# Building the adjacency matrices of a graph network: paired values for VectorE, degree sums as rows of one PSUM bank, ranks carried by groups of four tiles

## The chip, the cores and the metric

The kernel runs on one core of a Trainium2 chip. The metric is the device time of one execution in microseconds (us). TensorE (PE), VectorE (DVE), ScalarE (ACT), GpSimd (POOL) and SyncE (SP) run side by side and wait for each other by semaphores.

## The reference

Four graph layers are applied in turn to 6250 nodes of 128 features, with 106250 directed edges sorted by destination:

```
x = _layernorm(x + _L0_gnn_ref(x, edge_index, edge_attr_64, ...))   # message MLP per edge, summed per node, GRU
x = _layernorm(x + _L1_gnn_ref(x, edge_index, ...))                 # deg^-1/2 normalized sum over edges and reversed edges
x = _layernorm(x + _L2_gnn_ref(x, edge_index, ...))                 # the same over edges
x = _layernorm(x + _L3_gnn_ref(x, edge_index, edge_weight, ...))    # three weighted convolutions
```

A layer of this kind is a product of a node-by-node matrix with the features, scaled by powers of the nodes' degrees:

```
deg = jax.ops.segment_sum(w, dst, num_segments=n_nodes)
msg = m[src] * norm[:, None]
out = jax.ops.segment_sum(msg, dst, num_segments=n_nodes)
```

## The kernel before

The nodes make NB = 49 blocks of 128. One stage builds, once, three dense matrices (edge counts, reversed counts, edge weights) block row by block row, stores them in HBM, and later stages multiply with them. The change lies in this building stage, which runs from about 60 to about 1600 us; it also carries the first graph layer (one gather of node rows, one small product and one sum for each of 208 steps of 512 edges), woven between the block work at places that are fixed in the code (`at_place`, `tick`).

For block row u, DVE and PE sort the edges of the block (at most 20 tiles of 128 edges) so that each edge stands alone in a slot of its pair k of source blocks (NK = 25 pairs):

- `sort_keys(u)` (L617, L619) marks for every edge its pair: `in_pair`, 20 tiles by 26.
- `ranks(u)` on PE (L778, L780) counts, for each edge, the earlier edges of its pair: one product with a triangle, then 19 products that carry the sum of tile t to all later tiles.
- `sort_ranks(u)` on DVE (L626 to L640) makes `at_rank` (where each edge goes) and `spread` (its five values times `in_pair`, L634).
- `sort(u)` on PE (L788) moves them to their slots; `sort_out(u)` on DVE (L646 to L652) reads the result into `slots`.
- `one_hots(u, h)` on DVE builds for the two halves h of the pairs the one-hot matrices: `hot_s` of the sources (L665, 25 instructions a row), `hot_d` of the destinations (L670), and for u >= NARROW = 16 three weighted ones `hot_w` (L677). `hot_d` and `hot_w` lie in the room called `rows_a` in the profile.
- `blocks(n)` on PE takes one or two pairs a step, 13 steps a row. For each pair: products for the matrices (L814, L817), and sums for the degrees with the one-hots as the stationary operand and 1 or 4 columns moving (L815, L819). For u >= 16 twelve products more for the weights (L834).
- ACT takes each PSUM bank to SBUF (L904, L909), SP stores it. There are three banks (`ps_mat`) and three staging buffers.

The rows u < 16 ("narrow") leave out the forward counts and the weights; the rows u >= 16 are called wide here. First-layer work on the same engines: POOL gathers rows of `p_table` (L925, four for each step, eight steps ahead at most), PE multiplies (L844) and sums (L857), DVE adds and places (L685, L689, L697, L698), ACT applies ReLU (L914). Each engine works its own list in the order of the code.

Of the kernel before, what the change touches and what calls it, by code (L numbers as in the profile page):

```python
# [59 lines left out]
FAR = 1e6  # L60
assert CHUNKS * CB == NB and CHKS * CHK == NB and E <= T * P and HS * TH == T and HS % 2 == 0
# [48 lines left out]
def per_row(col, n):  # L110

    return col.unsqueeze(2).to_broadcast([col.shape[0], col.shape[1], n])

# [12 lines left out]
def build(nc, a, out):  # L126
    with ExitStack() as ctx:
# [43 lines left out]
        zero = sb("zero", [P, 64 + 4 * NB])  # L171
# [55 lines left out]
        with ExitStack() as c:  # L227
# [14 lines left out]
            with ExitStack() as c0:  # L242
# [50 lines left out]
                with nc.Block() as block:  # L293
# [67 lines left out]
                    def _(dve):  # L361
# [32 lines left out]
                        chain.step(V.tensor_scalar(vals[:, :, 1], dst_row[:], 1.0, None, ALU.add))  # L394
# [33 lines left out]
                        chain.step(V.tensor_tensor(vals[:, :, 0], tmp_f[:], src_f[:], ALU.subtract))  # L428
# [83 lines left out]
            spread = sb("spread", [P, VT, NV, NK + 1], BF16, c)  # L512

            slots = sb("slots", [P, 2, NV + 1, NK + 1], BF16, c)
# [10 lines left out]
            hot = sb("hot", [P, 4, TH, W], F32, c)  # L525
            st_cnt = sb("st_cnt", [P, STAGES, 2, 4 * P], BF16, c)
            st_wt = sb("st_wt", [P, STAGES, 4 * P], F32, c)
            deg_in = sb("deg_in", [P, NB, 4], F32, c)
            deg_out = sb("deg_out", [P, NB], F32, c)
            self_c = sb("self_c", [P, NB], F32, c)  # L530
            self_w = sb("self_w", [P, NB], F32, c)
            deg = sb("deg", [P, 4, NB], F32, c)
# [8 lines left out]
            hot_d_ready, source_ready = sem("hot_d_ready"), sem("source_ready")  # L541
            hots_ready, filled, evicted = sem("hots_ready"), sem("filled"), sem("evicted")
# [62 lines left out]
            with nc.Block() as block:  # L605
                @block.vector
                def _(dve):
# [5 lines left out]
                    def sort_keys(u):  # L613
# [6 lines left out]
                                        ALU.is_equal).then_inc(pair_ready, 1)  # L620

                    def sort_ranks(u):
# [11 lines left out]
                        V.tensor_tensor(spread[:], in_pair[:].unsqueeze(2).to_broadcast([P, VT, NV, NK + 1]),  # L634
                                        vals[:, at, :].unsqueeze(3).to_broadcast([P, VT, NV, NK + 1]),
# [64 lines left out]
                    def tick():  # L700
# [3 lines left out]
                        if e is not None:  # L704
                            if e < HS:
                                message_sum(e)
                            if e >= 4 and e % 2 == 0:
                                add_sums((e - 4) // 2)

                    sort_keys(0)  # L710
                    sort_ranks(0)
                    sort_out(0)
# [1318 lines left out]
```

## Time and profile before

| | us |
|---|---|
| median of 3 runs | 4412.11 (4409.29 to 4418.47) |
| profiled execution, its own time | 4412.28 |
| its span | 4410.5 |
| PE busy | 3810.4 (86%) |
| DVE busy | 2944.6 (67%) |
| POOL busy | 2815.0 (64%) |
| ACT busy | 1529.5 (35%) |

Shares of the whole span average over stages with different limits; the building stage is about a third of the span and has to be read by itself. A matmul's recorded duration holds its way through the array, so the pace of PE is read from the starts of its instructions.

In a row of the windows stand the stretch, its length, busy us (and instructions) of PE, PE's weight loads, DVE, ACT and POOL, TensorE's granted clock (1.00 is 2.4 GHz, 0.50 is 1.2 GHz), the share of the DMA engines and GB/s. In a row of groups: busy us, mean ns of one, idle us ahead of them and what ended it. In a row of a timeline: start and duration in us.

### The profile page before, as it was taken

The page shows a single profiled execution, that of the slowest core. Times are in us where ns is not written, and L with a number is a line of the kernel's source. Part 1 is how long each engine was busy: PE and PEld are TensorE (multiplying, and loading weights), DVE is VectorE, ACT ScalarE, POOL GpSimd, SP SyncE. Part 2 cuts the span into 40 slices and gives each one's busy share as a digit, 9 for nine tenths or more (in the row PEclk, how much of TensorE's full clock was granted, in tenths as well). Part 3 has the DMA queues.
Part 4 walks back from the last instruction along what each step waited for, and adds up shares of the span by engine and source line. Part 5 has one row for each costly group of instructions (what it writes and reads, how often), then busy time and mean ns, then how long its engine had stood idle before and what let it go on. Part 6 is the DMA issues. An engine that isn't in the chain of part 4 may idle for free. (4 is left out here: it accounts for less than half of the span.)

```text
span 4410.5 us, 83016 instructions
## 1 busy us (share of the span) xinstructions
PE 3810.4 (86%) x30818; PEld 2546.0 (58%) x30818; DVE 2944.6 (67%) x6093; ACT 1529.5 (35%) x3170; POOL 2815.0 (64%) x2363
## 2 busy tenths in 40 slices
PE   5887999998988865688987986999899999998998
PEld 4766888887878754344444443455445555554444
DVE  8899999999999868355553344466356666523665
ACT  3334566665656546000000000333134444412332
POOL 3876888888888810566635774777266666606773
PEclk7778999998999977899998998999999999998999
DMA  4444777777777753999976775999655555537997
GB/s 140 133 126 133 231 247 240 238 237 225 248 236 238 228 201 115 290 322 322 323 260 211 240 233 167 329 323 327 219 204 195 185 199 191 193 109 278 331 318 263
DMA packets 612904, 1019.51 MB, mean 231 GB/s; under 512 B 90888, under 2 KB 417575, under 8 KB 612111
## 3 DMA queue, kind: packets, MB, share of 16 engines
q1 hardware_dynamic: 476700, 773.91, 51.5%
q0 software_dynamic: 90848, 199.74, 15.3%
q10 hardware_dynamic: 44956, 40.55, 2.8%
q8 instruction: 247, 4.05, 0.4%
q14 instruction: 153, 1.25, 0.1%
HBM read 737.12 MB, written 276.78 MB: 230 GB/s over the span
## 5 line engine op out<-in xcount | busy, mean ns | idle before, releaser
L925 POOL DMA_INDIRECT x<-p_table,src_i x832 | 1218.5, 1464 | 344.5 <-issue 241.8
L1514 POOL DMA_INDIRECT rows_b<-x_table,low_src x552 | 574.9, 1041 | 485.1 <-POOLq L144 206.4
L1514 POOL DMA_INDIRECT rows_a<-h_table,low_src x412 | 448.1, 1088 | 240.1 <-DVE split_l3b L1805 120.4
L904 ACT CAST st_cnt<-ps_mat 128x512 bf16<-128x512 f32 (+1 forms) x825 | 440.9, 590 | 444.5 <-PE ps_deg L819 384.3
L1593 PE MATMUL po_l3b<-mat_l3b,rows_b 128*128 128x512 f32 (+1 forms) x1372 | 570.9, 564 | 19.6 <-DMA mat_l3b<-weights_fwd 18.6
L1593 PE MATMUL po_l3a<-mat_l3a,rows_a 128*128 128x512 f32 (+1 forms) x882 | 375.0, 572 | 30.0 <-DMA mat_l3a<-weights_fwd 29.3
L1593 PE MATMUL po_l3c<-mat_l3c,rows_a 128*128 128x512 f32 (+1 forms) x882 | 375.3, 573 | 13.9 <-DMA mat_l3c<-weights_fwd 13.2
L1593 PE MATMUL po_l<-mat_l,rows_a 128*128 128x512 bf16 (+1 forms) x1323 | 296.2, 380 | 99.8 <-DVE mat_l L1833 99.0
L1593 PEld LDWEIGHTS po_l3b<-mat_l3b,rows_b 128*128 128x128 f32 x1372 | 241.6, 195 | 241.5 <-issue 221.1
L834 PE MATMUL ps_mat<-rows_a,hot_s 128*128 128x128 bf16 x4851 | 360.8, 226 | 9.0
L677 DVE TENSOR_TENSOR rows_a<-rows_a,slots 128x1792 bf16<-128x1792 bf16 (+1 forms) x198 | 366.8, 1886 | 1.4
L1514 POOL DMA_INDIRECT rows_a<-x_table,low_src x276 | 285.7, 1035 | 93.3 <-issue 84.5
L1514 POOL DMA_INDIRECT rows_a<-m_table,low_src x276 | 276.9, 1003 | 90.2 <-issue 85.0
L814 PE MATMUL ps_mat<-rows_a,hot_s 128*128 128x128 bf16 x1617 | 255.5, 224 | 88.0 <-DVE rows_a L677 64.7
L1748 ACT ACTIVATE t_l<-y_l 128x512 f32<-128x512 f32 (+1 forms) x26 | 15.7, 605 | 887.7 <-DVE y_l L1888 887.7
L817 PE MATMUL ps_mat<-hot_s,rows_a 128*128 128x256 bf16 x1225 | 321.8, 284 | 0.0
L834 PEld LDWEIGHTS ps_mat<-rows_a,hot_s 128*128 128x128 bf16 x4851 | 291.2, 101 | 46.2 <-ACT st_wt L909 34.8
L1593 PE MATMUL po_l<-mat_l,rows_b 128*128 128x512 bf16 (+1 forms) x1323 | 289.2, 374 | 19.3 <-DMA mat_l<-counts_fwd 18.4
L815 PE MATMUL ps_deg<-slots,hot_s 128*128 128x1 bf16 x2401 | 283.7, 168 | 22.7 <-issue 13.3
L844 PE MATMUL pm<-w1eT,rows_a 65*128 65x128 f32 x1664 | 254.3, 300 | 13.9 <-DVE x L689 13.8
L1593 PEld LDWEIGHTS po_l<-mat_l,rows_a 128*128 128x128 bf16 x1323 | 123.8, 102 | 242.4 <-DVE mat_l L1833 112.3
L1593 PEld LDWEIGHTS po_l3a<-mat_l3a,rows_a 128*128 128x128 f32 x882 | 157.9, 196 | 176.2 <-issue 145.6
(415 smaller groups left out, 7448.8 us busy)
## 6 DMA issues: line engine op xcount, KB each, us to landing
weights_fwd<-st_wt SPq DMA_DIRECT2D x396, 256.0 KB
mat_l<-counts_fwd SPq DMA_DIRECT2D x112, 896.0 KB
mat_l3a<-weights_fwd SPq DMA_DIRECT2D x56, 1792.0 KB
mat_l3c<-weights_fwd SPq DMA_DIRECT2D x56, 1792.0 KB
counts_rev<-st_cnt SPq DMA_DIRECT2D x588, 128.0 KB
rev_l<-counts_rev SPq DMA_DIRECT2D x84, 896.0 KB
mat_l3b<-weights_fwd SPq DMA_DIRECT2D x42, 1792.0 KB
counts_fwd<-st_cnt SPq DMA_DIRECT2D x396, 128.0 KB
```

Of the source, the lines that this page charges most:

```text
L677: V.tensor_tensor(hot_w[:, h, v, 0:n, :], hot_d[:, h, 0:n, :], per_row(slots[:, u % 2, 2 + v, ks], P), ALU.mult).then_inc(hots_ready, 1)
L814: nc.tensor.matmul(ps_mat[:, b, q * P:(q + 1) * P], half, rows, start=True, stop=True)
L815: nc.tensor.matmul(ps_deg[:, 2 * k + q:2 * k + q + 1], half, slots[:, u % 2, NV, k:k + 1], start=False, stop=False)
L817: nc.tensor.matmul(ps_mat[:, b, rev_at:rev_at + len(halves) * P], rows, hot_s[:, h, j0 + j, 0:len(halves) * P], start=True, stop=True)
L834: mm = nc.tensor.matmul(ps_mat[:, f % 3, (2 * j + q) * P:(2 * j + q + 1) * P], half, hot_w[:, h, v, j0 + j, :], start=(v == 0), stop=(v == 2))
L844: mm = nc.tensor.matmul(pm[:, j % 2, t * FD:(t + 1) * FD], edge[:, i % 2, (h * TH + t) * P:(h * TH + t + 1) * P], w1eT[:], start=True, sto ...
L904: nc.scalar.copy(st_cnt[:, q, :, j * 2 * P:j * 2 * P + n_col], ps_mat[:, f % 3, :].rearrange("p (d c) -> p d c", d=2)[:, :, 0:n_col]).then ...
L925: pool.indirect_dma_start(ring[:, j % RING, t * FD:(t + 1) * FD], None, p_table, bass.IndirectOffsetOnAxis(src_i[:, j * TH + t:j * TH + t ...
L1514: pool.indirect_dma_start(ring[:, j % RL, t, :], None, table, bass.IndirectOffsetOnAxis(low_src[:, j * TH + t:j * TH + t + 1].bitcast(U32), 0)
L1593: mm = nc.tensor.matmul(po[:, p % 2, k, 0:nb * P].rearrange("p (d c) -> p d c", c=P), rows[:, s, k * P:(k + 1) * P], cols, start=(s == 0 a ...
L1748: nc.scalar.activation(t1[:, 0:nb, 0:FD], y2[:, f % ys, 0:nb], ACT.Square).then_inc(act_out, 1)
```

## The change

Five edits, all in the building stage.

1. `hot_d`, `hot_w` and `spread` multiply or compare a tile with a value that is the same for a whole row. Before, that value is read with a step of zero, element by element. Now each value lies twice side by side (`slots` and `vals_2` hold every value two times), and the operand is read as pairs of neighbours.
2. The degree sums. Before, the one-hot matrix is stationary and one or four columns move, and each sum is a column of `ps_deg`. Now a small matrix `marks` is stationary (its k+1 or 4 row+4 columns are zero but for the last ones), the one-hot matrices move (256 and 128 columns), and each sum is a row of `ps_deg`. `marks` is filled by a new copy for each half row and zeroed once.
3. The ranks. DVE sums `in_pair` over groups of four tiles (`group_sum`), and PE carries inside the groups by three products and from group to group by four.
4. At the end of the stage ACT copies `ps_deg` to SBUF and PE turns it by four small products; DVE reads the turned sums.
5. The order of the five values changes, and some buffers share room.

```
 def twice(col):
     return col.unsqueeze(len(col.shape)).to_broadcast([*col.shape, 2])
 def in_pairs(tile):
     return tile.rearrange("p n (c e) -> p n c e", e=2)
 def per_row_pairs(pairs, n):
     return pairs.unsqueeze(2).to_broadcast([pairs.shape[0], pairs.shape[1], n // 2, 2])
...
+                        dve.wait_ge(pair_ready, u + 1)
+                            V.tensor_reduce(group_sum[:], in_pair[:, 0:VT - 4, 0:NK].rearrange("p (g t) k -> p g k t", t=4),
+                                            AX.X, ALU.add).then_inc(groups_ready, 1)
...
+                        V.tensor_copy(vals_2[:], twice(vals[:, at]))
...
-                        V.tensor_tensor(spread[:], in_pair[:].unsqueeze(2).to_broadcast([P, VT, NV, NK + 1]),
-                                        vals[:, at, :].unsqueeze(3).to_broadcast([P, VT, NV, NK + 1]),
+                        V.tensor_tensor(spread[:].rearrange("p t v (k e) -> p t v k e", e=2),
+                                        in_pair[:].rearrange("p t (k e) -> p t k e", e=2).unsqueeze(2).to_broadcast(
+                                            [P, VT, NV, (NK + 1) // 2, 2]),
+                                        vals_2[:].unsqueeze(3).to_broadcast([P, VT, NV, (NK + 1) // 2, 2]),
                                         ALU.mult).then_inc(lots_ready, 1)
...
-                        V.tensor_copy(slots[:, u % 2, 0:NV, :], found).then_inc(slots_ready, 1)
+                        V.tensor_copy(slots[:, u % 2], twice(found)).then_inc(slots_ready, 1)
...
-                        V.tensor_scalar(slots[:, u % 2, NV, :], slots[:, u % 2, 1, :], 0.0, None,
+                        V.tensor_scalar(slots[:, u % 2, 1], slots[:, u % 2, 0], 0.0, None,
                                         ALU.is_gt).then_inc(slots_ready, 1)
...
-                        V.tensor_tensor(hot_d[:, h, 0:n, :], per_block(iota_up[:], n), per_row(slots[:, u % 2, 1, ks], P),
+                        dve.wait_ge(slots_ready, 2 * u + 2)
+                        V.tensor_copy(marks[:, ks.start:min(ks.stop, NK), LEAD:], slots[:, u % 2, 1:NV, ks.start:min(ks.stop, NK), 0].rearrange(
+                            "p v k -> p k v")).then_inc(marks_ready, 1)
+                        V.tensor_tensor(in_pairs(hot_d[:, h, 0:n, :]), in_pairs(per_block(iota_up[:], n)),
+                                        per_row_pairs(slots[:, u % 2, 0, ks], P),
                                         ALU.is_equal).then_inc(hot_d_ready, 1)
...
-                            V.tensor_tensor(hot_w[:, h, v, 0:n, :], hot_d[:, h, 0:n, :],
-                                            per_row(slots[:, u % 2, 2 + v, ks], P), ALU.mult).then_inc(hots_ready, 1)
+                            V.tensor_tensor(in_pairs(hot_w[:, h, v, 0:n, :]), in_pairs(hot_d[:, h, 0:n, :]),
+                                            per_row_pairs(slots[:, u % 2, 2 + v, ks], P), ALU.mult).then_inc(hots_ready, 1)
...
+                    V.memset(marks[:], 0.0).then_inc(marks_ready, 1)
...
-                        for t in range(VT - 1):
-                            mm = nc.tensor.matmul(at[:, t + 1:VT, :], ones_b[:],
-                                                  in_pair[:, t:t + 1, 0:NK].to_broadcast([P, VT - 1 - t, NK]),
-                                                  start=False, stop=(t == VT - 2))
+                        at_4, pair_4 = (v.rearrange("p (g t) k -> p g t k", t=4) for v in (at, in_pair[:, :, 0:NK]))
+                        for d in range(1, 4):
+                            nc.tensor.matmul(at_4[:, :, d:4, :], ones_b[:], pair_4[:, :, 0:4 - d, :], start=False, stop=False)
+                        pe.wait_ge(groups_ready, u + 1)
+                        for g in range(VT // 4 - 1):
+                            mm = nc.tensor.matmul(at[:, 4 * g + 4:VT, :], ones_b[:],
+                                                  group_sum[:, g:g + 1, :].to_broadcast([P, VT - 4 * g - 4, NK]),
+                                                  start=False, stop=(g == VT // 4 - 2))
...
-                                nc.tensor.matmul(ps_deg[:, 2 * k + q:2 * k + q + 1], half, slots[:, u % 2, NV, k:k + 1],
-                                                 start=False, stop=False)
...
-                            mm = nc.tensor.matmul(ps_deg[:, 64 + 4 * u:68 + 4 * u], rows, slots[:, u % 2, 2:NV + 1, k],
-                                                  start=False, stop=False)
+                            both = hot_s[:, h, j0 + j, 0:len(halves) * P]
+                            nc.tensor.matmul(ps_deg[0:k + 1, 0:len(halves) * P], marks[:, k, LEAD - k:LEAD + 1], both,
+                                             start=False, stop=False)
+                            nc.tensor.matmul(ps_deg[0:4 * row + 4, (2 + part) * P:(3 + part) * P],
+                                             marks[:, k, LEAD - 4 * row:LEAD + 4], rows, start=False, stop=False)
...
+                    nc.scalar.copy(deg_sums, ps_deg[:]).then_inc(degs_copied, 1)
```

What TensorE does for the first pair of a wide row, before (the names are the tile written, then the two operands; the shape is that of the moving operand):

```order
L814 MATMUL ps_mat<-rows_a,hot_s 128x128
L815 MATMUL ps_deg<-slots,hot_s 128x1
L814 MATMUL ps_mat<-rows_a,hot_s 128x128
L815 MATMUL ps_deg<-slots,hot_s 128x1
L817 MATMUL ps_mat<-hot_s,rows_a 128x256
L819 MATMUL ps_deg<-slots,rows_a 128x4
```

and at the same place after (block row 16; the first number of a shape on `marks` is the number of its columns that are stationary):

```order
L854 MATMUL ps_deg<-hot_s,marks 1x256
L856 MATMUL ps_deg<-rows_a,marks 68x128
L860 MATMUL ps_mat<-rows_a,hot_s 128x128 x2
L862 MATMUL ps_mat<-hot_s,rows_a 128x256
L854 MATMUL ps_deg<-hot_s,marks 2x256
```

Six products a pair became five, and the degree sums moved ahead of the matrix products, with 384 moving columns where there were 6.

The ranks on TensorE, before (first rows of 20):

```order
L778 MATMUL ps_sort<-in_pair,tri_b 128x500
L780 MATMUL ps_sort<-in_pair,ones_b 128x475
L780 MATMUL ps_sort<-in_pair,ones_b 128x450
L780 MATMUL ps_sort<-in_pair,ones_b 128x425
L780 MATMUL ps_sort<-in_pair,ones_b 128x400
```

and after, all of them:

```order
L816 MATMUL ps_sort<-in_pair,tri_b 128x500
L819 MATMUL ps_sort<-in_pair,ones_b 128x5x75
L819 MATMUL ps_sort<-in_pair,ones_b 128x5x50
L819 MATMUL ps_sort<-in_pair,ones_b 128x5x25
L822 MATMUL ps_sort<-group_sum,ones_b 128x400
L822 MATMUL ps_sort<-group_sum,ones_b 128x300
L822 MATMUL ps_sort<-group_sum,ones_b 128x200
L822 MATMUL ps_sort<-group_sum,ones_b 128x100
```

Twenty products of 5250 columns became eight of 2250, and the last four wait for a sum that VectorE makes.

On VectorE, the end of the first half's one-hots and the start of the next row's sort, before (square brackets name the semaphores that a row waits for):

```order
L677 TENSOR_TENSOR rows_a<-rows_a,slots 128x1792 x2
L685 TENSOR_TENSOR hot<-iota_row,local 128x256 [waits step_sum]
L689 TENSOR_TENSOR x<-pm,x 128x512 [waits edge_mul,gathered3]
L626 TENSOR_TENSOR picked<-in_pair,ps_sort 128x500 [waits pair_ready,ranked]
L628 TENSOR_REDUCE rank<-picked 128x20 [waits b_dve]
```

and after (`vals<-vals` is the copy into `vals_2`):

```order
L712 TENSOR_TENSOR rows_a<-rows_a,slots 128x1792 x2
L720 TENSOR_TENSOR hot<-iota_row,local 128x256 [waits step_sum]
L724 TENSOR_TENSOR x<-pm,x 128x512 [waits edge_mul,gathered3]
L654 ISA [waits pair_ready,ranked]
L654 COPY vals<-vals 128x200
L655 TENSOR_TENSOR picked<-in_pair,ps_sort 128x500
L657 TENSOR_REDUCE rank<-picked 128x20 [waits b_dve]
```

The old instructions keep their order and their sizes; copies are set in between, here behind the wait for the ranks.

## Rows read from the trace of the kernel before

**Rows 1.** Windows: the narrow block rows, then the wide ones

```profile
60.00:425.00 365.00, 286.32 (x2959) 237.78 (x2960) 327.57 (x848) 130.61 (x250) 271.87 (x200) 0.78 0.43 124
425.00:1590.00 1165.00, 1055.85 (x13547) 951.19 (x13545) 1084.47 (x2088) 705.94 (x1405) 945.54 (x632) 0.93 0.74 235
```

**Rows 2.** Who waited for whom, 425 to 1590 us: us, times, longest

```profile
ACT st_cnt L904 <- PE ps_deg L819: 384.3, 192, 8.3
...
PE ps_mat L814 <- DVE rows_a L677: 64.7, 29, 5.7
ACT st_cnt L904 <- DMA weights_fwd<-st_wt: 46.9, 45, 2.7
...
DVE key L617 <- issue: 21.0, 31, 1.5
...
DVE acc L697 <- issue: 16.2, 21, 1.4
PE ps_mat L814 <- ACT st_cnt L904: 14.9, 41, 2.2
DVE x L689 <- DMA x<-p_table,src_i: 14.1, 10, 2.5
...
PE pm L844 <- DVE x L689: 11.5, 9, 3.0
...
PE ps_mat L814 <- DVE hot_s L665: 5.4, 9, 1.4
```

**Rows 3.** Groups of DVE by shape, 425 to 1590 us: busy us, mean ns | idle

```profile
L677 DVE TENSOR_TENSOR rows_a<-rows_a,slots 128x1792 bf16<-128x1792 bf16 x98 | 194.4, 2019 | 0.6
L677 DVE TENSOR_TENSOR rows_a<-rows_a,slots 128x1536 bf16<-128x1536 bf16 x99 | 170.3, 1753 | 0.8
...
L634 DVE TENSOR_TENSOR spread<-in_pair,vals 128x2600 bf16<-128x2600 bf16 x32 | 91.5, 2861 | 0.0
...
L631 DVE TENSOR_TENSOR at_rank<-num_r,rank_b 128x2560 bf16<-128x2560 bf16 x32 | 47.7, 1492 | 1.1
...
L628 DVE TENSOR_REDUCE rank<-picked 128x20 f32<-128x500 f32 x32 | 21.6, 674 | 1.1
...
L646 DVE CAST slots<-ps_sort 128x130 bf16<-128x130 f32 x32 | 9.2, 287 | 0.0
```

**Rows 4.** Groups of POOL, the same stretch

```profile
L925 POOL DMA_INDIRECT x<-p_table,src_i x632 | 945.5, 1496 | 200.6 <-issue 183.9 <-DVE x L689 16.7
```

**Rows 5.** Timeline of DVE and of POOL near 1040 us: start, us

```profile
1038.49 1.75 DVE L670 TENSOR_TENSOR rows_a<-iota_up,slots 128x1536 bf16<-128x1536 bf16 x1
...
1038.56 2.50 POOL L925 DMA_INDIRECT x<-p_table,src_i  x1 [0.30 <-issue]
1041.37 0.94 POOL L925 DMA_INDIRECT x<-p_table,src_i  x1 [0.30 <-issue]
```

**Rows 6.** Timeline of PE: ranks, then steps, then a first-layer piece

```profile
1018.11 0.38 PE L778 MATMUL ps_sort<-in_pair,tri_b 128*128 128x500 bf16 x1
...
1020.51 0.22 PE L814 MATMUL ps_mat<-rows_a,hot_s 128*128 128x128 bf16 x1
...
1020.80 0.22 PE L814 MATMUL ps_mat<-rows_a,hot_s 128*128 128x128 bf16 x1
...
1021.77 0.22 PE L814 MATMUL ps_mat<-rows_a,hot_s 128*128 128x128 bf16 x1
...
1023.34 1.11 PE L844 MATMUL pm<-w1eT,rows_a 65*128 65x128 f32 x8
```

**Rows 7.** Groups of DVE by shape, 60 to 425 us

```profile
L634 DVE TENSOR_TENSOR spread<-in_pair,vals 128x2600 bf16<-128x2600 bf16 x17 | 48.6, 2860 | 0.0
L670 DVE TENSOR_TENSOR rows_a<-iota_up,slots 128x1792 bf16<-128x1792 bf16 x17 | 34.2, 2015 | 0.0
...
L670 DVE TENSOR_TENSOR rows_a<-iota_up,slots 128x1536 bf16<-128x1536 bf16 x16 | 28.0, 1748 | 0.0
...
L626 DVE TENSOR_TENSOR picked<-in_pair,ps_sort 128x500 f32<-128x500 bf16 x17 | 11.4, 669 | 13.8 <-PE ps_sort L780 13.8
```

More of the change, by code:

```diff
@@ L60 @@
 FAR = 1e6
+DEG_BLOCKS = -(-NB // 2)
+LEAD = 4 * (DEG_BLOCKS - 1)
 assert CHUNKS * CB == NB and CHKS * CHK == NB and E <= T * P and HS * TH == T and HS % 2 == 0
@@ L112, in per_row, with twice, in_pairs, per_row_pairs @@
     return col.unsqueeze(2).to_broadcast([col.shape[0], col.shape[1], n])
+def twice(col):
+    return col.unsqueeze(len(col.shape)).to_broadcast([*col.shape, 2])
+def in_pairs(tile):
+    return tile.rearrange("p n (c e) -> p n c e", e=2)
+def per_row_pairs(pairs, n):
+    return pairs.unsqueeze(2).to_broadcast([pairs.shape[0], pairs.shape[1], n // 2, 2])
 def per_block(row, k):
@@ L512, in build @@
             spread = sb("spread", [P, VT, NV, NK + 1], BF16, c)
-            slots = sb("slots", [P, 2, NV + 1, NK + 1], BF16, c)
+            vals_2 = sb("vals_2", [P, VT, NV, 2], BF16, c)
+            slots = sb("slots", [P, 2, NV, NK + 1, 2], BF16, c)
             source = sb("source", [P, 2, NK + 1], F32, c)
@@ L620, in sort_keys @@
                                         ALU.is_equal).then_inc(pair_ready, 1)
+                        dve.wait_ge(pair_ready, u + 1)
+                        with nc.allow_low_precision(reason="whole numbers up to four"):
+                            V.tensor_reduce(group_sum[:], in_pair[:, 0:VT - 4, 0:NK].rearrange("p (g t) k -> p g k t", t=4),
+                                            AX.X, ALU.add).then_inc(groups_ready, 1)
                     def sort_ranks(u):
@@ L799, in blocks @@
                         pe.wait_ge(hot_d_ready, m + 1)
-                        if s == 0:
-                            pe.wait_ge(slots_ready, 2 * u + 2)
+                        pe.wait_ge(marks_ready, m + 2)
+                        part, row = divmod(u, DEG_BLOCKS)
                         for j, k in enumerate(sub_pairs(s)):
@@ L886, in _ @@
                             first_layer(u, s)
-                    nc.tensor.matmul(ps_deg[:, 0:DEG], zero[:, 0:P], zero[:, 0:DEG], start=False, stop=True).then_inc(filled, 1)
+                    nc.tensor.matmul(ps_deg[:], zero[:, 0:P], no_sums, start=False, stop=True).then_inc(filled, 1)
+                    pe.wait_ge(evicted, fills_before(NB))
+                    pe.wait_ge(degs_copied, 1)
+                    for part in range(2):
+                        n = 4 * min(DEG_BLOCKS, NB - part * DEG_BLOCKS)
+                        nc.tensor.matmul(ps_mat[:, 0, 4 * DEG_BLOCKS * part:4 * DEG_BLOCKS * part + n],
+                                         deg_sums[0:n, (2 + part) * P:(3 + part) * P], ident[0:n, 0:n], start=True, stop=True)
+                    for q in range(2):
+                        n = NK - (2 * NK > NB and q)
+                        mm = nc.tensor.matmul(ps_mat[:, 1, q:q + 2 * n - 1:2], deg_sums[0:n, q * P:(q + 1) * P],
+                                              ident[0:n, 0:n], start=True, stop=True)
+                    mm.then_inc(degs_turned, 1)
                     pe.wait_ge(count_ready, 1)
@@ L1053, in _ @@
                         act.wait_ge(turned, 1)
-                        nc.scalar.copy(deg_rows[:], ps_mat[0:2 * NB, 0, 0:P]).then_inc(turn_read, 1)
+                        nc.scalar.copy(deg_rows, ps_mat[0:2 * NB, 0, 0:P]).then_inc(turn_read, 1)
                         act.wait_ge(root_in, 1)
```

66 lines of the change are left out of this document (37 added, 29 removed).

## The prediction

> **What bounds the kernel now.** I read the windows first. The building stage is two stretches: 365 us with 16 narrow block rows (some 22 us each, the start included) and 1165 us with 33 wide ones (35.3 us each) [rows 1]. In the wide stretch DVE is busy 1084 of 1165 us, 93%. PE shows 1056, but its durations overlap; ACT is busy 61%, the DMA engines 74%. POOL is busy 946 and idle 201, of which 184 are the 0.30 us between two gathers in which it waits for nobody [rows 4]: 632 x (1.496 + 0.305) = 1138 us, so POOL never rests either.
>
> The waits tell who is late. PE waits for DVE at L814 and L844, 65 + 12 + 5 = 82 us, and for ACT 15 us; DVE waits for a gather only 14 us, and its other idle time (21 + 16 us) is the reading of registers [rows 2]. ACT's 384 us behind PE are its slack. So DVE sets the pace of the wide rows, with POOL 27 us behind it. In the narrow stretch DVE is busy 328 of 365 us, and 14 of the rest are waits for the ranks [rows 1, 7].
>
> **Why DVE and POOL are tied.** Near 1040 us DVE runs L670 for 1.75 us; a gather that POOL starts 0.07 us later takes 2.50 us, and the next one 0.94 [rows 5]: 1.75 - 0.07 + 0.82. So a gather that meets a long two-input operation of DVE waits for its end. The mean of 1.496 us [rows 4] is 0.94 and 0.56 of such waiting. Shorter operations on DVE therefore make POOL faster too.
>
> The Trainium skill ("SBUF — State Buffer", Who interferes with whom) says that a Vector instruction with two SBUF inputs contends with a GpSimd instruction that reads SBUF, and infers that descriptor generation is not held up by it. The first half fits the 2.50 us, the second does not; if it held for these gathers, they would keep their 1.496 us.
>
> **Edit 1, pairs.** Per element, L677 costs (2019 - 1753) / 256 = 1.04 ns, with 157 ns fixed [rows 3]. `at_rank` (L631) has both inputs with neighbours side by side and takes 1.492 us for 2560 elements, 0.52 ns each [rows 3]. No row has a pair repeated 64 times. Upper bound: nothing gained, 2.02 us stays. Lower bound: L631's rate, 157 + 1792 x 0.52 = 1.09 us, 0.96 for 1536, 1.51 for `spread`. I take the lower one: the old operand is a repeated element too and runs at the full 1.04 ns, so repeating costs nothing.
> - Wide: L677 98 x 0.93 + 99 x 0.79 = 169 us; L670, at the durations of [rows 7] and 33 of each, 0.92 x 33 + 0.79 x 33 = 56; `spread` 32 x 1.35 = 43 [rows 3]. Together 268.
> - Narrow: 17 x 0.92 + 16 x 0.79 + 17 x 1.35 = 51 us [rows 7].
>
> **What DVE gets in return**, per block row: the group sum reads 400 elements; L628 reads 500 in 0.674, so 0.57 us if its strided reading is free, and I allow 1.1 at twice that; the copy to `vals_2`, 200 elements, 0.25 (L646 takes 0.287 for 130 out of PSUM, so 0.36 at most); `slots` written twice, 130 elements more than L646's 0.287, 0.14; two copies of about 50 elements to `marks`, 0.2 each by the same row; waits and the doubled comparison 0.1. Sum 1.5 us (up to 2.1): 49 us wide, 25 narrow. Zeroing `marks` (2500 columns) is up to 2.6 us once. DVE's wide work falls by 268 - 49 = 219 to about 946 us for the stretch, idle time included. So DVE stops being the bound, and what comes next has to be found.
>
> **POOL next?** The waiting of a gather goes as the sum of squared durations of the two-input operations over the row's time. Per wide row that sum was 4 x (2.02² + 1.75²) + 2.86² + 1.49² + 1.6 (small ones) = 41; it becomes 4 x (1.09² + 0.96²) + 1.51² + 1.49² + 1.6 = 14.6. Even in a row 9% shorter the waiting falls to 0.39 of 0.56 = 0.22 us: 632 x (0.94 + 0.22 + 0.305) = 926 us. POOL does not bind.
>
> **PE is next** (edits 2 and 3). The ranks take 20 products, 1018.11 to 1020.51, 2.40 us for 5250 columns [rows 6]. Now 8 products of 2250 columns, 0.43 of it, 1.03 us; 31 rows x 1.37 = 43 us. Part of this time was used by ACT to catch up, so I count 32. For each pair, six products from 1020.51 took 0.29 us to the next pair's first at 1020.80 [rows 6]. At 2.40 us / 5250 = 0.457 ns per column the new pair's 896 columns are 0.41 us at most, and 0.37 at 2.4 GHz; 0.08 more in 816 pairs, 68 us, if nothing hides it. But ACT hides most: the first step after the ranks takes 1.26 us (1020.51 to 1021.77), the second 1.57 (to 1023.34) [rows 6], since ACT must first empty a bank. Two such steps with 0.16 us more each are 2.84 us instead of 2.83. A row has 13 steps and about 7 pieces between them (5 of the first layer, one sort, one ranks), so some two or three steps a row stand alone and pay: 2.5 x 0.16 x 33 = 13 us.
>
> The wide stretch is then 1165 - 82 (waits for DVE) + 17 (a rest of them, since DVE at 946 is near) - 32 + 13 - 18 = 1063 us. The 18 are for the clock: granted 0.93 [rows 1], so 14% of the stretch, 163 us, ran at 1.2 GHz after PE had waited; the most that this can give back is half of it, 82 us, the least nothing; I take 18, since much of it lies beside waits that are counted already, and since PE will still wait now and then. So -102.
>
> **Narrow rows.** DVE 51 - 25 = 26 us less; of the 14 us of waits for ranks half goes, 7; the zeroing takes 2.6 back; and PE, at a clock of 0.78 there [rows 1], has 640 moving columns for each pair where it had 262, for which I take 10 back. -20 us.
>
> **The end** (edit 4): a copy of 512 columns on ACT, four small products and two copies, all beside some 13 us of DVE's own work behind the same semaphore. Nothing; if it were all on the path, 2 us.
>
> Sum, against the profiled execution's 4412.3 (the median is 4412.1): 4412 - 102 - 20 = 4290; I say 4288.
>
> **The rivals.**
> - ACT and the stores hold the wide rows. ACT already waits 47 us for stores to land [rows 2], and DMA engines busy 0.74 go above 0.8. Then the ranks give nothing and a quarter of PE's 82 us of waits for DVE turns into waits for ACT, so 60 are left: 4412 - 60 - 20 = 4332. Chance 0.13.
> - Repeated pairs cost something: the operations take the middle of the two bounds, 1.55 us. DVE saves 134 - 49 = 85 us wide and nothing narrow, and the zeroing costs 2.6: 4330. Against it stands the free repeat of one element today. Chance 0.08. The Trainium skill ("Vector Engine (DVE) Microarchitecture Reference", Measured stream behaviour) says that a port keeps its rate only for runs of two adjacent 4-byte words, 1.73 instead of 1.05 ns otherwise. By that figure a product would take some 1.7 us; a pair of two-byte values is one such word.
> - Gathers keep 1.496 us: POOL binds at 1138 of 1165, total 4412 - 27 - 20 = 4365. Against it: the 2.50 and 0.94 us. Chance 0.05.
> - DVE's bound is all there is, PE follows: wide 946 + 25, total 4200. Chance 0.04.
> - Slower, and the change not doing what it says: pairs run at 1.04 ns an element as before. Then DVE, the bound, has 1.5 us more in each of 49 rows and 2.6 once: 4412 + 76 = 4488. It decides once the pairs save less than a fifth (49 of 268). L631 speaks against it. Chance 0.06.
>
> **How the numbers follow.** My forecast has 0.62, with its own range 4225 to 4330 (cost of the group sum, clock, ACT's share). 0.02 is left for no change. 0.2% of this time, 9 us, is about what a measurement can tell. The range 4225 to 4350 leaves out the slower case, the POOL case, the lowest and some of my own. Faster 0.92, same 0.02, slower 0.06.
>
> **What would show it.** L677's successor at 1.09 us (1792) and `spread` at 1.51. Gathers at a mean near 1.15. DVE busy near 80% in the wide rows, with waits for PE's `filled`; PE's waits for DVE under 20 us, its clock over 0.95. A wide row near 32 us, a narrow one near 20. Wrong would be: products over 1.3 us, PE's new degree products spaced wider than their columns, or ACT's waits for stores beyond 100 us.

## The result and the profile after

The changed kernel takes 4379.22 us, median of 4 runs (4375.57 to 4382.22); the kernel before, on the same chip, takes 4415.2 (4409.29 to 4418.47). The ratio is 0.9922, interval 0.9906 to 0.9938: 0.8% faster where 2.8% was forecast, and outside the range on its upper side. The profiled execution took 4380.14 us, its span is 4378.0.

By its interval the kernel is faster, but by less than the 2% that this study calls faster.

First the windows of the changed kernel, narrow rows and wide ones, with the columns of [rows 1]:

```profile
60.00:400.00 340.00, 328.46 (x2339) 205.00 (x2340) 301.08 (x914) 133.98 (x247) 220.77 (x199) 0.96 0.45 131
400.00:1560.00 1160.00, 1156.71 (x12482) 915.54 (x12479) 873.38 (x2219) 754.72 (x1418) 713.32 (x632) 1.00 0.75 238
```

In the wide rows DVE fell from 93% [rows 1] to 75% busy and POOL from 81% to 61%. PE went from 1056 of 1165 to 1157 of 1160 us, at a granted clock of 1.00. The bound has moved to PE, and PE has more to do than DVE had. Its waits, 400 to 1560 us (us, times, longest), are gone:

```profile
PE ps_deg L854 <- ACT st_cnt L958: 1.8, 4, 0.8
PE ps_deg L854 <- DVE rows_a L704: 0.7, 1, 0.7
PE ps_deg L854 <- ACT st_wt L963: 0.2, 1, 0.2
```

The groups of DVE by shape and of POOL, same stretch, which answer to [rows 3] and [rows 4]:

```profile
L712 DVE TENSOR_TENSOR rows_a<-rows_a,slots 128x1792 bf16<-128x1792 bf16 x98 | 103.0, 1084 | 0.6
L712 DVE TENSOR_TENSOR rows_a<-rows_a,slots 128x1536 bf16<-128x1536 bf16 x99 | 91.3, 955 | 0.8
L663 DVE TENSOR_TENSOR spread<-in_pair,vals 128x2600 bf16<-128x2600 bf16 x32 | 48.1, 1504 | 0.0
L647 DVE TENSOR_REDUCE group_sum<-in_pair 128x100 bf16<-128x400 bf16 x31 | 25.9, 835 | 1.1
L677 DVE CAST slots<-ps_sort 128x260 bf16<-128x260 f32 x32 | 13.6, 426 | 19.7 <-PE ps_sort L830 15.8 <-issue 3.8
L980 POOL DMA_INDIRECT x<-p_table,src_i x632 | 713.3, 1129 | 377.6 <-DVE x L724 203.1 <-issue 174.5
```

The pairs take 1084, 955 and 1504 ns, within a hundredth of a us of the lower bound, and the gathers 1129 ns. POOL now waits 203 us for a free buffer. So DVE and POOL did what was forecast. PE did not. The stationary operand of a product is the one that PE loads ahead of it (the weight load, PEld in the profile); the other one is the moving operand, and its columns set how long the product streams. The timeline of PE in two pieces: the degree products have 13 and 8 stationary columns in the first, 7 and 36 in the second (start, us; the first number behind the names is partitions by stationary columns, the next the moving shape):

```profile
771.85 0.28 PE L854 MATMUL ps_deg<-hot_s,marks 128*13 128x256 bf16 x1
771.97 0.22 PE L856 MATMUL ps_deg<-rows_a,marks 128*8 128x128 bf16 x1
772.12 0.28 PE L860 MATMUL ps_mat<-rows_a,hot_s 128*128 128x128 bf16 x2
772.24 0.27 PE L862 MATMUL ps_mat<-hot_s,rows_a 128*128 128x256 bf16 x1
772.44 0.28 PE L854 MATMUL ps_deg<-hot_s,marks 128*14 128x256 bf16 x1
...
1003.87 0.27 PE L854 MATMUL ps_deg<-hot_s,marks 128*7 128x256 bf16 x1
1004.07 0.23 PE L856 MATMUL ps_deg<-rows_a,marks 128*36 128x128 bf16 x1
1004.23 0.28 PE L860 MATMUL ps_mat<-rows_a,hot_s 128*128 128x128 bf16 x2
1004.36 0.27 PE L862 MATMUL ps_mat<-hot_s,rows_a 128*128 128x256 bf16 x1
1004.56 0.27 PE L854 MATMUL ps_deg<-hot_s,marks 128*8 128x256 bf16 x1
```

Read the starts. A pair takes 0.59 us in the first piece and 0.69 in the second; before it took 0.29 [rows 6], and 0.41 was the forecast's most. Where a product of 256 moving columns is followed by one of like width the next start is 0.12 us later (771.85 to 771.97, 13 to 8 columns). Where the width goes from 7 to 36 it is 0.20 (1003.87 to 1004.07). The same 0.20 stands behind L862 (772.24 to 772.44, 1004.36 to 1004.56), where 128 stationary columns are followed by 8 or 14. The weight loads of the same two pieces say why (start, us, stationary columns):

```profile
771.86 0.09 PEld L856 LDWEIGHTS ps_deg<-rows_a,marks 128*8 128x8 bf16 x1
772.12 0.11 PEld L860 LDWEIGHTS ps_mat<-rows_a,hot_s 128*128 128x128 bf16 x2 [0.17 <-issue]
772.19 0.10 PEld L862 LDWEIGHTS ps_mat<-hot_s,rows_a 128*128 128x128 bf16 x1
...
1004.07 0.09 PEld L856 LDWEIGHTS ps_deg<-rows_a,marks 128*36 128x36 bf16 x1
1004.23 0.11 PEld L860 LDWEIGHTS ps_mat<-rows_a,hot_s 128*128 128x128 bf16 x2
1004.30 0.10 PEld L862 LDWEIGHTS ps_mat<-hot_s,rows_a 128*128 128x128 bf16 x1
1004.56 0.08 PEld L854 LDWEIGHTS ps_deg<-hot_s,marks 128*8 128x8 bf16 x1 [0.16 <-ACT st_wt L963]
```

Of like width, a load runs while the product ahead still streams: the load for the product at 771.97 begins at 771.86, that for 1004.36 at 1004.30. Of another width (8 to 128 at 772.12, 7 to 36 at 1004.07, 128 to 8 at 1004.56) load and product have the same start: the load is not taken ahead, and both start some 0.09 us late. The delay lies ahead of the load's start, so it is not the length of the load; what PE does in it the trace does not show. The widths need not be equal: over all block rows the spacing behind L854 has a median of 113 ns when both widths are 32 or less, and 206 ns when the second is above 32. There seem to be three classes of width (up to 32, up to 64, above 64), and the pair of `marks` columns crosses them two or three times. The experiments were made to test this.

The trace of the changed kernel has every width from 4 to 100 in steps of four, so it also shows where the classes end (medians of the spacing of starts in ns, over the pairs of wide rows that have another pair right behind them; e3 and e4 are explained below):

| columns of L856 | L854 to L856 | L856 to L860 | L862 to the next L854 | the pair |
|---|---|---|---|---|
| 4 to 32 | 113 | 152 | 202 | 590 |
| 36 to 64 | 206 | 164 to 176 | 202 | 695 to 707 |
| 68 to 100 | 206 | 82 to 95 | 202 | 602 to 616 |
| 128 or 100 for both (e3, e4) | 109 | 56 | 109 | 386 |

One border lies between 32 and 36 columns and the other between 64 and 68. The timeline on both sides of the second:

```profile
1291.27 0.24 PE L856 MATMUL ps_deg<-rows_a,marks 128*64 128x128 bf16 x1
1291.44 0.28 PE L860 MATMUL ps_mat<-rows_a,hot_s 128*128 128x128 bf16 x2
...
1325.25 0.24 PE L856 MATMUL ps_deg<-rows_a,marks 128*68 128x128 bf16 x1
1325.33 0.27 PE L860 MATMUL ps_mat<-rows_a,hot_s 128*128 128x128 bf16 x2
```

The table shows a second, smaller cost. Behind a product whose own load was not taken ahead, the next start is later by about 0.4 ns for each of its stationary columns (82 ns with 68 columns, 95 with 100, where 56 is the spacing of hidden loads); with 128 columns it is only 10 ns later (66 instead of 56 between the two L860 of the first two lines).

The ranks, in the timeline of the same kernel: the first of the eight products and what follows the last, 1.10 us apart (2.40 before, [rows 6]).

```profile
501.92 0.38 PE L816 MATMUL ps_sort<-in_pair,tri_b 128*128 128x500 bf16 x1
...
503.02 0.28 PE L854 MATMUL ps_deg<-hot_s,marks 128*21 128x256 bf16 x1
```

The Trainium skill ("TensorE: Matmul & The Clock Gate", Step-by-step: what each phase is for) says that TensorE pulls the load of a stationary operand ahead of running products when their row groups do not conflict, or when the load goes to the background weight buffer. It names no condition on the number of stationary columns for this, and all these products use 128 rows, so by that page nothing tells one of these loads from another. The trace shows loads taken ahead for like width (771.86 for the product at 771.97) and not for the others (772.12 for the product at 772.12): the measurement decides.

### The profile page after: what moved, and what is told of

It is laid out like the page before. It is cut to its first block and busy times, and to the rows that moved or that the text cites. A ratio compares the mean times of both kernels' runs of the same rounds, so it can differ in the third digit from the quotient of the medians.

```text
span 4378.0 us, 80386 instructions
## 1 busy us (share of the span) xinstructions
PE 3946.3 (90%) x29062; PEld 2471.1 (56%) x29062; DVE 2706.7 (62%) x6290; ACT 1577.2 (36%) x3171; POOL 2538.0 (58%) x2363
## 5 line engine op out<-in xcount | busy, mean ns | idle before, releaser
L980 POOL DMA_INDIRECT x<-p_table,src_i x832 | 935.3, 1124 | 545.7 <-DVE x L724 257.2
L958 ACT CAST st_cnt<-ps_mat 128x512 bf16<-128x512 f32 (+1 forms) x825 | 454.4, 578 | 380.7 <-PE ps_mat L862 358.8
L854 PE MATMUL ps_deg<-hot_s,marks 128*1 128x256 bf16 (+4 forms) x1225 | 336.5, 275 | 6.0 <-DVE rows_a L704 3.4
L877 PE MATMUL ps_mat<-rows_a,hot_s 128*128 128x128 bf16 x4851 | 340.9, 219 | 0.0
L862 PE MATMUL ps_mat<-hot_s,rows_a 128*128 128x256 bf16 x1225 | 336.3, 275 | 0.0
L877 PEld LDWEIGHTS ps_mat<-rows_a,hot_s 128*128 128x128 bf16 x4851 | 305.4, 98 | 4.5
L856 PE MATMUL ps_deg<-rows_a,marks 128*4 128x128 bf16 (+24 forms) x1225 | 290.2, 237 | 0.0
L696 DVE TENSOR_SCALAR hot_s<-iota,source 128x256 bf16<-128x256 bf16 x1225 | 253.0, 293 | 38.9 <-PE ps_mat L877 37.8
L1756 ACT ACTIVATE split_l3b<-rows_a,low_weight 128x256 bf16<-128x256 f32 x412 | 175.4, 496 | 213.8 <-DMA rows_a<-h_table,low_src 146.5
```

Of the source, the lines that this page charges most:

```text
L696: V.tensor_scalar(hot_s[:, h, j, :], iota_256[:], source[:, u % 2, k:k + 1], None, ALU.is_equal).then_inc(hots_ready, 1)
L854: nc.tensor.matmul(ps_deg[0:k + 1, 0:len(halves) * P], marks[:, k, LEAD - k:LEAD + 1], both, start=False, stop=False)
L856: nc.tensor.matmul(ps_deg[0:4 * row + 4, (2 + part) * P:(3 + part) * P], marks[:, k, LEAD - 4 * row:LEAD + 4], rows, start=False, stop=False)
L862: mm = nc.tensor.matmul(ps_mat[:, b, rev_at:rev_at + len(halves) * P], rows, both, start=True, stop=True)
L877: mm = nc.tensor.matmul(ps_mat[:, f % 3, (2 * j + q) * P:(2 * j + q + 1) * P], half, hot_w[:, h, v, j0 + j, :], start=(v == 0), stop=(v == 2))
L958: nc.scalar.copy(st_cnt[:, q, :, j * 2 * P:j * 2 * P + n_col], ps_mat[:, f % 3, :].rearrange("p (d c) -> p d c", d=2)[:, :, 0:n_col]).then ...
```

## The experiments

Each run was made beside the kernel before on its chip. Runs e1 to e4 share one chip (before: 4427.18 us), e5 to e8 another (4940.8), e9 to e12 a third (4412.07). "First to last ranks" is the time from the start of the first product of the ranks to that of the last (block row 0 to 48): 1465.8 us before, 1435.3 after.

| run | us, median | ratio (interval) | first to last ranks |
|---|---|---|---|
| changed kernel | 4379.22 | 0.9922 (0.9906 to 0.9938) | 1435.3 |
| e1 pairs and ranks, degrees as before | 4269.7 | 0.9629 (0.9591 to 0.9667) | 1330.5 |
| e2 pairs only | 4273.18 | 0.965 (0.9616 to 0.9684) | 1326.5 |
| e3 marks 128 wide | 4254.36 | 0.961 (0.9576 to 0.9644) | 1312.2 |
| e4 marks 100 wide | 4248.69 | 0.9598 (0.957 to 0.9627) | 1309.4 |
| e9 marks grouped | 4295.25 | 0.9742 (0.971 to 0.9774) | 1354.8 |
| e10 single values | 4464.47 | 1.0126 (1.0093 to 1.016) | 1514.8 |
| e11 e1, stationary cut to 32 | 4717.04 | 1.0717 (1.0673 to 1.0762) | 1761.5 |
| e12 e1, stationary cut to 96 | 4267.88 | 0.9685 (0.9643 to 0.9727) | 1319.9 |

**Which edit takes the gain back.** e1 is the changed kernel with the degree sums of before: one and four moving columns, the one-hots stationary, no `marks`, no turning.

```
-  nc.tensor.matmul(ps_deg[0:k + 1, 0:len(halves) * P], marks[:, k, LEAD - k:LEAD + 1], both, ...)
-  nc.tensor.matmul(ps_deg[0:4 * row + 4, (2 + part) * P:(3 + part) * P], marks[:, k, LEAD - 4 * row:LEAD + 4], rows, ...)
+  nc.tensor.matmul(ps_deg[:, 2 * k + q:2 * k + q + 1], half, slots[:, u % 2, 1, k, 0:1], ...)     # for each q
+  nc.tensor.matmul(ps_deg[:, 64 + 4 * u:68 + 4 * u], rows, slots[:, u % 2, 1:NV, k, 0], ...)
```

Expected:

> The changed kernel with the degree sums as before: the one-hot matrices stationary, 1 or 4 columns of slots moving, no marks, no copy and turn at the end; pairs for VectorE and grouped ranks stay. Theory (the narrow stationary marks cost PE 0.69 us a pair where its columns say 0.37): a pair is back at 0.29 to 0.31 us, the wide rows fall from 35.3 to about 32 us, the total to 4255 to 4290. Rival (what holds the changed kernel is something else that the pairs brought, as ACT's evictions or the stores): the time stays within 20 us of the changed kernel's 4379.

Measured: 4269.7 us, ratio 0.9629, inside the range of the theory. Without edit 2 the kernel is 3% faster than with it.

e2 is edit 1 alone: the degree sums and the 20 products of the ranks as before.

```
-  for d in range(1, 4): ...   # grouped ranks, and group_sum on DVE
+  for t in range(VT - 1):
+      mm = nc.tensor.matmul(at[:, t + 1:VT, :], ones_b[:], in_pair[:, t:t + 1, 0:NK].to_broadcast([P, VT - 1 - t, NK]), ...)
```

Expected:

> The kernel before with edit 1 alone (values twice side by side); ranks and degree sums as before. Theory: PE's 82 us of waits for VectorE go for the most part, 4285 to 4310, 20 to 40 us above the same with grouped ranks. Rival (VectorE's shorter operations were worth nothing by themselves): within 20 us of 4412.

Measured: 4273.18 us, ratio 0.965. That is below the expected 4285 to 4310, and 3.5 us above e1 where 20 to 40 were expected; the intervals of e1 and e2 overlap. So the grouped ranks (edit 3) give nothing that can be told, and edit 1 alone gives 3.5%. The windows of e1 and, below it, of e2 from 400 to 1400 us show where the ranks' gain stays:

```profile
400.00:1400.00 1000.00, 939.27 (x12484) 851.32 (x12482) 816.68 (x2048) 665.71 (x1328) 712.13 (x623) 0.96 0.82 262
```
```profile
400.00:1400.00 1000.00, 953.13 (x12845) 851.97 (x12841) 796.69 (x2027) 665.59 (x1330) 699.84 (x623) 0.99 0.82 262
```

PE is busy 14 us less in e1, and ACT and the DMA engines have done the same work in the same time, so something beside PE's work sets the pace. The waits of e1 (380 to 1470 us) point to ACT and the stores:

```profile
ACT st_cnt L940 <- PE ps_deg L855: 234.5, 140, 8.7
ACT st_cnt L940 <- DMA weights_fwd<-st_wt: 102.3, 92, 3.2
```

ACT waits 102 us for stores to leave a staging buffer, where it waited 47 [rows 2]. PE's clock is a second candidate: 0.96 was granted in e1's stretch and 0.99 in e2's, so part of what the grouped ranks save may come back as slower products. No run separates the two.

**Is it the number of columns, or the change of width?** e3 keeps edit 2, but gives every product on `marks` a stationary operand of 128 columns, mostly zeros: the same 384 moving columns a pair, wider loads, and no change of width. Some small tiles share room with others to make place for the wider `marks`.

```
-  LEAD = 4 * (DEG_BLOCKS - 1)
+  LEAD = DEG_BLOCKS - 1;  WIDE = 128
-  nc.tensor.matmul(ps_deg[0:k + 1, ...], marks[:, k, LEAD - k:LEAD + 1], both, ...)
-  nc.tensor.matmul(ps_deg[0:4 * row + 4, ...], marks[:, k, LEAD - 4 * row:LEAD + 4], rows, ...)
+  nc.tensor.matmul(ps_deg[0:WIDE, ...], marks[:, k, LEAD - k:LEAD - k + WIDE], both, ...)
+  nc.tensor.matmul(ps_deg[0:WIDE, ...], marks[:, k, LEAD - row:LEAD - row + WIDE], rows, ...)
```

Expected:

> The changed kernel with marks stationary always 128 columns wide (152 columns kept for each pair, the four values 25 columns apart, the sums in rows v*25+row), everything else as in the change; picked shares the room of at_rank. Theory A (a weight load is exposed where the width of the stationary operand changes between up to 32, up to 64 and more columns): a pair takes 0.37 to 0.40 us, total 4270 to 4310. Theory B (a load of marks between one-hot matrices is exposed whatever its width): a pair stays near 0.69 us, total 4370 to 4390.

e4 is the same with `WIDE = 100`: it tells whether full width is needed.

> The same as the kernel with 128 columns, but 100 columns of marks stationary, for both degree products. Theory A1 (only the class of the width matters, over 64): within 10 us of the kernel with 128 columns. Theory A2 (a load of other than 128 columns also takes longer, by 0.41 ns a column as the changed kernel's products with 68 to 100 columns show): some 0.04 us for each of two or three loads of a pair, 20 to 60 us above it. Theory B: 4370 to 4390.

Measured: 0.961 and 0.9598. The timeline of PE in e3, one pair:

```profile
1001.76 0.27 PE L858 MATMUL ps_deg<-hot_s,marks 128*128 128x256 bf16 x1
1001.87 0.22 PE L860 MATMUL ps_deg<-rows_a,marks 128*128 128x128 bf16 x1
1001.92 0.28 PE L864 MATMUL ps_mat<-rows_a,hot_s 128*128 128x128 bf16 x2
1002.04 0.27 PE L866 MATMUL ps_mat<-hot_s,rows_a 128*128 128x256 bf16 x1
1002.14 0.27 PE L858 MATMUL ps_deg<-hot_s,marks 128*128 128x256 bf16 x1
```

A pair takes 0.38 us (1001.76 to 1002.14), which is what its columns cost at 2.4 GHz (896 / 2.4 = 373 ns). So of the 0.40 us by which the pair of 1003.87 was longer than that of [rows 6], 0.09 come from more moving columns and 0.31 from the changes of width: three late starts of 0.09 us, and the rest from the loads themselves, by the table above. The total, 4254.36 us, is below both ranges that were given; the pair of 0.38 us is what theory A said. The weight loads of e3 run ahead again:

```profile
1001.76 0.10 PEld L860 LDWEIGHTS ps_deg<-rows_a,marks 128*128 128x128 bf16 x1
1001.87 0.15 PEld L864 LDWEIGHTS ps_mat<-rows_a,hot_s 128*128 128x128 bf16 x2
```

They start at 1001.76 and 1001.87, for products that start at 1001.87 and 1001.92. The window of e3 shows the kernel without the changes of width: PE 96% busy, the DMA engines 0.83 of the time, 265 GB/s.

```profile
400.00:1400.00 1000.00, 959.52 (x11937) 888.05 (x11935) 835.78 (x2149) 679.76 (x1349) 711.98 (x624) 0.99 0.83 265
```

e4, a mixture of 100 and 128 columns, loses nothing against e3 (4246.51 to 4254.68 us against 4247.04 to 4266.48). So it is no matter of equal widths, nor of full ones, and theory A2 (20 to 60 us above e3) fails. The Trainium skill ("TensorE: Matmul & The Clock Gate", Weight-path perf modes) says that the fast weight load is on when the number of weights is 128 and the type is not FP32. The 10 ns of a bare load of 128 columns against 26 to 39 of one of 68 to 100 agree with that. If it were what made the changed kernel slow, e4 would have lost as much; its pair takes 386 ns, as that of e3.

**Does the order help?** e6 and e9 are one kernel: the two L854 of a step first, then the two L856, then the matrix products (L848, L851, L866 and L868 in its own timeline). That halves the changes of width into and out of `marks`.

```
+  for first in (True, False):
+      for j, k in enumerate(sub_pairs(s)):
+          ... the product with hot_s for both pairs, then that with rows_a for both
   for j, k in enumerate(sub_pairs(s)): ... the matrix products
```

e5 and e10 are the changed kernel without edit 1 (`hot_d`, `hot_w` and `spread` read single values again): what edits 2 and 3 are worth without the relief of DVE.

```
-  per_row_pairs(slots[:, u % 2, 2 + v, ks], P)
+  per_row(slots[:, u % 2, 2 + v, ks, 0], P)
```

e7 and e11 are e1 with the stationary operand of each degree product cut to its first 32 columns, e8 and e12 with it cut to 96. They leave out three quarters and one quarter of the entries of each degree sum.

```
-  nc.tensor.matmul(ps_deg[:, 2 * k + q:2 * k + q + 1], half, ...)
+  nc.tensor.matmul(ps_deg[0:32, 2 * k + q:2 * k + q + 1], half[:, 0:32], ...)      # and 0:96
```

These change the width at the products of before, where `marks`, its copies and the order of edit 2 are not there. What was expected of the four, first time:

> The changed kernel, but the three kinds of products of VectorE read each value singly as before (the doubled layout, the marks and the grouped ranks stay): edits 2 and 3 with all copies, without what the pairs gain. Theory: VectorE needs its old 35.5 us a wide row and 1.5 for the copies, PE its 35.4, so a wide row takes 37 to 38 us and a narrow one 22 to 23; total 4440 to 4500, slower than before. Rival (the copies hide, and PE's price was not felt beside VectorE's): 4400 to 4425.

> The changed kernel with the degree products of both pairs of a step issued together ahead of the step's matrix products: first the two with up to 25 columns of marks, then the two with 4 row+4. The same products, but three changes of the stationary operand's width in a step where there were six. Theory A (the change of width costs 0.09 us each): a wide row needs 12.5 x 0.28 = 3.5 us less PE time and ends near 32.5 us, since ACT's pace comes next; total 4265 to 4310. Rival (each load of marks costs, whatever stands next to it): unchanged, 4365 to 4390.

> The kernel with pairs, grouped ranks and the old degree products, but for these products (1 or 4 columns moving) only the first 32 columns of the one-hot matrices are stationary, so three quarters of each degree sum are left out. No marks anywhere; only the width of the stationary operand differs. Theory A: six changes of width a pair in the wide rows, 0.09 us each, 0.55 us more a pair, 11 to 14 us a row; total 4550 to 4720 though each load moves less. Rival (the price belongs to marks, to its strides or to the moving one-hots): 4235 to 4270, as with 128 columns.

> The same with 96 columns stationary in the degree products (a quarter of each sum left out): over 64 columns, but not 128. Theory A1 (only the class of the width counts): 4240 to 4275. Theory A2 (a load of other than 128 columns is also slower, 0.03 to 0.04 us as between the changed kernel's products with 68 to 100 columns and its next): 4280 to 4370.

Measured: 5004.72, 4996.08, 5413.27 and 5007.79 us, ratios 1.0154 (1.008 to 1.0229), 1.0128 (1.0057 to 1.0199), 1.0948 (1.0848 to 1.1048) and 1.0123 (1.0051 to 1.0195). All four times lie outside the ranges of every theory, and they are inconclusive as times: on that chip the kernel before took 4940.8 us where the other two chips gave 4427 and 4412, and one of the four, e8, is e1 cut to 96 and came out slower than before where the uncut kernel had been 3.7% faster elsewhere. What set the pace there I have not found out. The expectation for e9 names the stores, but the traces do not show it: in e6 the DMA engines are 0.58 busy from 400 to 1400 us, in e9 0.81. The spacings of starts could be used already, and all four were run again on another chip.

> The kernel with grouped marks once more, on another chip if there is one, since the call before measured even the kernel before at 4941 us, with the stores as the limit. Its trace has already shown 114 ns behind a product of 256 columns whose neighbour has marks of the same width class, and 202 where the class changes. Theory A: a wide row near 32.5 us, total 4265 to 4310 where the kernel before has 4412. Rival: 4365 to 4390.

> Edits 2 and 3 with every copy but single values, once more. Theory: VectorE binds again with 1.5 us more a row, 4440 to 4500 where the kernel before has 4412. Rival (PE and VectorE share the delay): 4500 to 4560. Or the copies hide: 4400 to 4425.

> The old degree products with 32 columns stationary, once more; its trace showed 109 ns behind a product of one column where the uncut one takes 26, and 159 where it takes 55. Theory A: 25 x 0.5 us a wide row more on PE, 4550 to 4720 where the kernel before has 4412.

> The same with 96 columns stationary; its trace showed the spacings of the uncut kernel (26 and 55 ns). Only the class counts: 4240 to 4275 where the kernel before has 4412.

Measured: all four times within what was expected, see the table. In the grouped order (e9) the timeline shows the two products of like width together:

```profile
1003.57 0.39 PE L848 MATMUL ps_deg<-hot_s,marks 128*11 128x256 bf16 x2
1003.88 0.29 PE L851 MATMUL ps_deg<-rows_a,marks 128*40 128x128 bf16 x2
1004.11 0.29 PE L866 MATMUL ps_mat<-rows_a,hot_s 128*128 128x128 bf16 x2
```

Order alone takes the ratio from 0.9922 to 0.9742, about half of the way to 0.9598.

The timelines of PE in e11 (cut to 32) and e12 (cut to 96) are the plainest reading of all:

```profile
1002.20 0.22 PE L850 MATMUL ps_mat<-rows_a,hot_s 128*128 128x128 bf16 x1
1002.35 0.18 PE L851 MATMUL ps_deg<-slots,hot_s 128*32 128x1 bf16 x1
1002.46 0.23 PE L850 MATMUL ps_mat<-rows_a,hot_s 128*128 128x128 bf16 x1
```
```profile
1000.84 0.22 PE L850 MATMUL ps_mat<-rows_a,hot_s 128*128 128x128 bf16 x1
1000.90 0.17 PE L851 MATMUL ps_deg<-slots,hot_s 128*96 128x1 bf16 x1
1000.93 0.22 PE L850 MATMUL ps_mat<-rows_a,hot_s 128*128 128x128 bf16 x1
```

With 32 columns the next start comes 0.15 us after the product of 128 moving columns and 0.11 after that of one; with 96 columns 0.06 and 0.03. The smaller stationary operand is the slower one, by 0.08 to 0.10 us each time (medians: 26 to 109 ns behind one moving column, 56 to 158 behind 128), in both directions. e12 is as fast as e1 as far as can be told (the intervals 0.9643 to 0.9727 and 0.9591 to 0.9667 just overlap), e11 is 7.2% slower than before. That takes `marks`, the moving columns, DVE's copies and the place of the degree sums out of the question: the change of width alone does it. The number of stationary columns is also the number of rows of PSUM that the product writes, and these runs change the two together; which of them PE goes by is open. In e11 a wide row rose from e1's 32.2 us to 41.7 (medians of the spacing of the ranks' starts).

e10, at 1.0126 (1.0093 to 1.016), shows that edits 2 and 3 with their copies, but without the relief of the pairs, make the kernel some 1.3% slower than before. Its window says that both engines are close to full, DVE 943 and PE 977 of 1000:

```profile
400.00:1400.00 1000.00, 977.17 (x10111) 763.66 (x10111) 943.11 (x1886) 611.38 (x1141) 807.00 (x550) 0.97 0.71 224
```

Its gathers take 1468 ns on average, near the 1496 of before [rows 4], where edit 1's kernels have 1129 (after) and 1144 (e1).

## Why the prediction was wrong

- **The failing step is a term of the sum that was mis-sized**: "At 2.40 us / 5250 = 0.457 ns per column the new pair's 896 columns are 0.41 us at most, and 0.37 at 2.4 GHz; 0.08 more in 816 pairs, 68 us, if nothing hides it." The new pair takes 0.59 to 0.71 us, 0.30 to 0.42 more than before. The columns are costed rightly (e3: 0.38 us); what is missing is two or three late starts a pair, 0.09 us each, since the stationary operand changes its class of width, and some 0.02 to 0.04 us for the loads that then lie bare. The rate that I took from [rows 6] comes from a run of products that all have 128 stationary columns. I named this as a sign of being wrong ("PE's new degree products spaced wider than their columns") but gave it no price and no rival. (33 rows of 25 pairs are 825 and not 816, which changes nothing.)
- **What followed from it**: "two or three steps a row stand alone and pay: 2.5 x 0.16 x 33 = 13 us". With 0.30 to 0.42 us a pair PE itself became the bound (1157 us busy of 1160, hardly a wait), so every step pays. From the last ranks ahead of the first wide row's products (399.15 us, before 416.83) to the last ranks of all (1496.5, before 1526.1) the wide rows gained 1109.3 - 1097.3 = 12 us, not 102. The step in which ACT hides most of the price goes with it: ACT waited 359 us for L862 and only 12 for stores, so it was PE that ACT waited for.
- **Pairs** (edit 1): 1.09, 0.96 and 1.51 us forecast, 1.084, 0.955 and 1.504 measured. Right. The rivals "cost something" and "1.04 ns an element" fall.
- **What DVE gets in return**: the group sum takes 0.84 us (0.57 taken, 1.1 allowed), `slots` 0.43 instead of the 0.29 of [rows 3] as forecast. Right within its bounds.
- **Gathers**: 1160 ns forecast (0.94 + 0.22), 1129 measured, and 1468 with single values in e10. Right, and so is the reason: a gather that starts more than 1 us ahead of the end of an L677 of before ends 0.82 us behind it (median of 53), as the one gather of [rows 5] did behind its operation. POOL does not bind. The rule on two SBUF inputs that the prediction cited from the Trainium skill ("SBUF — State Buffer", Who interferes with whom) holds in its first half. Its inference, that descriptor generation is not held up, does not hold for these gathers as whole instructions; which part of a gather waits is not shown.
- **Ranks**: 1.03 us forecast for eight products; in the changed kernel they go from 501.92 to 503.02 us, 1.10. Right. But e1 against e2 gives nothing measurable for the 32 us that I booked. The rival "ACT and the stores hold the wide rows" said this, and ACT's 102 us of waits for stores in e1 are the sign that the prediction named, though the lower clock of e1 may have its share. In the changed kernel that wait is 12 us, so the rival was not the cause of the miss.
- **Edit 1 was worth more than I thought**: of its own, 3.5% or 154 us (e2), where my terms for it make 82 - 17 + 18 + 20 = 103 us. By the starts of the ranks the wide rows of e2 take 102 us less than those of before (forecast 83) and the narrow ones 37 less (forecast 20). The clock is 0.99 in e2's stretch against 0.93 [rows 1]; I took 18 of at most 82 us for it. That the rest lies there is argued, not shown.
- **Narrow rows**: -20 us forecast, 416.83 to 399.15 = -17.7 measured. The sum is right by luck: with edit 1 alone (e2) these rows gain 37 us and with wide `marks` (e4) 36, so the terms are too low for what the pairs bring, and the changes of width, for which there is no term, take some 18 back.
- **The end** (edit 4): no loss that can be seen. DVE waits 11.4 us there for the last degree products, 8.4 before.

The best version is e4, edits 1 to 4 with `marks` 100 columns wide: 4248.69 us, 4.0% faster than before. Against e1 (4250.98 to 4277.27 us) the ranges touch: by the medians edit 2 done with wide `marks` is worth half a per cent, and it may be nothing; done as in the change it costs 3%.

## What to carry to other kernels

Price a stream of matmuls by the spacing of starts of products with the same stationary widths as the new ones, not by columns alone. Where narrow and wide stationary operands take turns, pad the narrow one with zeros into the class of its neighbours, or group the narrow ones: the padding cost nothing here (386 ns a pair, as its columns say), and the alternation 3.2% of the kernel. A value stored twice side by side nearly halves the time of an operation that spreads it along a row (2019 to 1084 ns for 1792 elements). The kernel gains by it as far as nothing else binds: here it freed DVE and POOL at once, 3.5% of the time in e2.

## What was not expected of the hardware

- A product whose stationary operand has another class of width than the one ahead starts 0.08 to 0.1 us late: behind a product of one moving column the next start comes after 26 ns (e1) or 109 (e11), behind 128 columns after 56 or 149, behind 256 after 109 or 202 (both in the changed kernel; medians of the spacing). Its load begins only when it does. 13 to 8, 96 to 128 and 100 to 128 columns are changes inside a class; 7 to 36, 36 to 128 and 32 to 128 are not. The borders lie between 32 and 36 and between 64 and 68 columns, the steps in which `marks` grows.
- The operand read as repeated pairs runs at 0.52 ns an element, like one without any repeat, though the same pair is read 64 times over ((1504 - 1084) / 808 ns).
- One of the three chips of the experiments ran every kernel more slowly: the kernel before by 12% (4940.8 against 4412.07 us), e5 to e8 by 12 to 17% against e9 to e12, though the spacings between products were nearly the same where PE's clock was full (e8 against e12: 28 and 26 ns behind one moving column, 56 and 56 behind 128, 109 and 108 behind 256).
